# A decoder layer on one core: in the last batch the two layer norms behind the second attention are made per token half

## The reference, cut to what matters

```python
def _layernorm(x, axis=-1, eps=1e-05):
    m = jnp.mean(x, axis=axis, keepdims=True)
    v = jnp.var(x, axis=axis, keepdims=True)
    return (x - m) / jnp.sqrt(v + eps)
...
    x = _layernorm(x + _L0_attn_ref(x, ...), axis=-1)            # block A, gives x1
    x = _layernorm(x + _L0_xattn_ref(x, ctx_2048, ...), axis=-1)  # block B, ends in o @ Wo, gives x2
    x = _layernorm(x + _L0_ffn_ref(x, ...), axis=-1)              # block C, gives the output
...
def _L0_ffn_ref(x, ...):
    result = jnp.einsum('bsd,od->bso', x, base_w) + base_b
    logits = jnp.einsum('bsd,ed->bse', x, router_w) + router_b
    # softmax of 8 experts, the two largest renormalised to a gate of 8 numbers per token
    mid = jnp.einsum('nd,edr->ner', xf, lora_A) * gate[:, :, None]
    return result + 2.0 * jnp.einsum('ner,erd->nd', mid, lora_B)
```

## Time and profile before

| | |
|---|---|
| time, median of 3 runs | 913.03 us (912.97 to 913.53) |
| the profiled execution | 913.3 us, of which its span in the trace is 911.2 us |
| mean granted TensorE clock | 0.986 of full speed |
| PE busy | 802.1 us, 88% of the span |
| DVE, ACT, POOL busy | 509.5, 326.4, 85.5 us |
| instructions | 22548 |

### The profile page before, as it was taken

How to read it: one execution, slowest core, us unless ns; L and a number is a source line. 1 busy time by engine, 2 the same in 40 slices (tenths; PEclk the granted TensorE clock), 3 DMA queues, 4 the chain that set the end, 5 groups by cost and what they waited for, 6 DMA issues and landing times.

```text
span 911.2 us, 22548 instructions
## 1 busy us (share of the span) xinstructions
PE 802.1 (88%) x10161; PEld 524.5 (58%) x10209; DVE 509.5 (56%) x1060; ACT 326.4 (36%) x424; POOL 85.5 (9%) x103
## 2 busy tenths in 40 slices
PE   3788878888998989988998989988998979999996
PEld 2466763477445864577445864577445864486443
DVE  4756584448745593748745593648745582435143
ACT  5534224333245224433245224433245124310422
POOL 1111011000300021000300021000300010010001
PEclk9989999999999999999999999999999999997998
DMA  9921000100002000010002000010001000000000
GB/s 345 246 55 47 2 2 1 47 2 2 2 1 70 3 2 1 26 47 2 1 1 71 3 2 1 27 46 1 1 1 48 2 1 1 24 1 1 1 24 23
DMA packets 19022, 27.10 MB, mean 30 GB/s; under 512 B 5608, under 2 KB 7784, under 8 KB 18928
## 3 DMA queue, kind: packets, MB, share of 16 engines
q1 hardware_dynamic: 18784, 25.64, 9.1%
q10 hardware_dynamic: 144, 0.03, 0.0%
HBM read 21.47 MB, written 4.19 MB: 28 GB/s over the span
## 4 chain that ended last, share of the span: by engine, by line
PE 63%; DVE 19%; ACT 12%; issue 4%; POOL 1%; DMA 1%; ACTq 0%; POOLq 0%; SPq 0%; DVEq 0%
ACT p_b L761 7%; PE ps L1148 7%; PE ps L1184 6%; PE ps L1065 6%; PE ps L1225 6%; DVE max_b L1487 6%; PE ps L1113 4%; PE ps L1048 3%; PE ps L1085 3%; PE ps L893 2%; DVE max_a L1385 2%; PE ps L968 2%; PE ps L1173 2%; PE ps L1157 2%; PE ps L978 2%
## 5 line engine op out<-in xcount | busy, mean ns | idle before, releaser
L761 ACT ACTIVATE p_b<-ps 128x2048 f32<-128x2048 f32 x64 | 106.5, 1664 | 115.9 <-PE ps L1157 115.9
L1487 DVE TENSOR_REDUCE max_b<-ps 128x4 f32<-128x768 f32 (+2 forms) x160 | 106.6, 711 | 31.1 <-PE ps L1127 19.3
L1363 DVE SCALAR_TENSOR_TENSOR nat<-ps,st_a,qkv_bias 128x512 f32<-128x512 f32 x48 | 35.7, 744 | 98.0 <-PE ps L893 96.8
L1113 PE MATMUL ps<-qk_b 32*128 32x192 f32 (+2 forms) x1024 | 65.5, 341 | 22.9 <-DVE max_b L1487 16.8
L1148 PE MATMUL ps<-qk_b 32*128 32x512 f32 (+1 forms) x512 | 66.2, 586 | 9.7 <-ACT p_b L761 5.2
L1113 PEld LDWEIGHTS ps<-qk_b 32*128 32x128 f32 x1024 | 46.2, 188 | 39.9 <-DVE max_b L1487 27.3
L1225 PE MATMUL ps<-base_t,x_t 128*128 128x512 f32 x128 | 63.8, 624 | 0.0
L1173 PE MATMUL ps<-p_b,v_b 128*32 128x256 f32 (+1 forms) x1024 | 61.7, 358 | 2.4 <-ACT p_b L761 2.0
L1048 PE MATMUL ps<-c_t,wq 128*128 128x256 f32 x256 | 60.6, 385 | 2.4 <-DVE out_a L1408 2.3
L1065 PE MATMUL ps<-x_t,wq 128*128 128x256 f32 x256 | 61.3, 385 | 0.0
L1184 PE MATMUL ps<-wo,o_fb 128*128 128x512 f32 x128 | 59.0, 599 | 0.8 <-DVE o_fb L1529 0.8
(11 more groups left out here) (207 smaller groups left out, 1432.7 us busy)
## 6 DMA issues: line engine op xcount, KB each, us to landing
x_in<-x SPq DMA_DIRECT2D x8, 512.0 KB, 5.4
p_b<-ctx SPq DMA_DIRECT2D x8, 512.0 KB, 4.6
y<-x SPq DMA_DIRECT2D x7, 512.0 KB, 3.3
p_b<-L_attn_qkv_w SPq DMA_DIRECT2D x2, 1024.0 KB, 6.5
p_b<-L_xattn_Wq SPq DMA_DIRECT2D x1, 2048.0 KB, 14.9
x<-L_attn_qkv_w SPq DMA_DIRECT2D x2, 512.0 KB, 9.5
x<-L_ffn_base_w SPq DMA_DIRECT2D x2, 512.0 KB, 10.2
wo<-L_xattn_Wo SPq DMA_DIRECT2D x8, 128.0 KB, 9.1
```

The costliest lines, as they stand in the source:

```text
L761: act.activation(p_b[:, j % 2, :, 0:cols], ps[:, 4:8, 0:cols], ACT.Exp, scale=DB ** -0.5).then_inc(pb_here.sem, 1)
L1113: pe.matmul(bank(4 + r)[:, (i % 2) * N:(i % 2) * N + 2 * n * S], q_b[strip[r], i, :, :].rearrange("p h q -> p (h q)"), k_b[strip[r], half, ...
L1363: dve.scalar_tensor_tensor(nat[:, t, w, :], bank(nat_bank(b, w)), st_a[:, 2, t:t + 1], qkv_bias[:, w * C:(w + 1) * C], ALU.mult, ALU.add). ...
L1487: ins = dve.tensor_reduce(max_b[:, half, 0, i:i + k, 2 * n:2 * n + 2], ps[:, 4 + 2 * n:6 + 2 * n, :].rearrange("p r (i n) -> p i r n", i=2 ...
```

## The change

Only batch 7 is changed (`alone(b)` is true for it). For the layer norms of blocks B and C, DVE makes bn_stats, bn_aggr and the variance for one half at a time (`half_stats`), POOL raises one half at a time, and DVE makes the shift of each half (`half_shift`). The order on DVE is now z of half 0, its statistics, then in block B the shift of half 0, z of half 1, its statistics, its shift; in block C z of half 1 stands ahead of the shift of half 0. ACT waits for each half alone, and copies the transposes of half 0 between the two norm applications of block B. PE makes both parts of the Wo product of half 0 ahead of those of half 1, transposes half t of x2 into bank 6 + t, and runs the router product of half 0 between the two groups of transposes. The `keep_on` products ahead of the transposes are 4 and 4, and were 14 and 2.

```diff
@@ POOL b4 (c2 is changed alike, with rs_c)
+                if alone(b):
+                    for t in range(T):
+                        vb_here(pool, b, t + 1)
+                        pool.tensor_tensor(rs_b[:, 1, t:t + 1], rs_b[:, 0, t:t + 1], neghalf[:, 0:1], ALU.pow).then_inc(rb_here.sem, 1)
+                    return
@@ ACT
-                    sh_here(act, b)
+                    sh_here(act, b, t + 1 if alone(b) else None)
...
-                sc_here(act, b)
                 for t in range(T):
+                    sc_here(act, b, t + 1 if alone(b) else None)
...
-                    act.activation(x2_t[:, :, t * P:(t + 1) * P], bank(1).rearrange("p (k n) -> p k n", k=KT),
+                    act.activation(x2_t[:, :, t * P:(t + 1) * P], bank(6 + t if alone(b) else 1).rearrange("p (k n) -> p k n", k=KT),
@@ PE c1_x2, c1
-                    keep_on(b, NB - 1, 2 if t else 14)
+                    keep_on(b, NB - 1, 4)
                     x2_here(pe, b, t + 1)
-                    if t:
+                    if alone(b):
+                        pb_here(pe, b)
+                    elif t:
                         x2t_here(pe, b, 1)
...
-                        mm = pe.transpose(bank(1)[:, k * P:(k + 1) * P], x2[:, t, k * P:(k + 1) * P], eye)
+                        mm = pe.transpose(bank(6 + t if alone(b) else 1)[:, k * P:(k + 1) * P], x2[:, t, k * P:(k + 1) * P], eye)
...
                 keep_on(b, NB - 1, 2)
-                x2t_here(pe, b)
+                if alone(b):
+                    outa_here(pe, b)
+                x2t_here(pe, b, t + 1 if alone(b) else None)
@@ DVE, new helpers
+            def half_stats(c, b, t, z, mv, rs, row, here):
+                c.start(dve, b, 2 * t)
+                c.link(dve.bn_stats(stats[:, t, :], z[:, t, :]))
+                c.link(dve.bn_aggr(mv[:, t, :], stats[:, t, :]))
+                dve.tensor_scalar(rs[:, row, t:t + 1], mv[:, t, 1:2], EPS_LN, None, ALU.add).then_inc(here.sem, 1)
+
+            def half_shift(b, t, mv, rs, row, rstd, done):
+                rstd(dve, b, t + 1)
+                dve.scalar_tensor_tensor(rs[:, row + 2, t:t + 1], mv[:, t, 0:1], -1.0, rs[:, row + 1, t:t + 1], ALU.mult, ALU.mult).then_inc(done.sem, 1)
@@ DVE list, block B and block C of batch 7
-                    (7, of(b4, 0)), (7, of(b4_z, 1)), (7, of(b4, 1)), (7, of(b4, 2)), (7, b4_x2), (7, c1), (7, of(c1_top, 0)), (7, of(c1_top, 1)),
+                    (7, of(b4, 0)), (7, of(b4, 2)), (7, of(b4_z, 1)), (7, of(b4, 1)), (7, b4_x2), (7, c1), (7, of(c1_top, 0)), (7, of(c1_top, 1)),
```

More of the change, by code:

```diff
@@ L411, in program, with alone @@
         NEXT, A, B, C_, D_ = -1, 0, 1, 2, 3
+        def alone(b):
+            return isinstance(b, int) and b == NB - 1
         def apart(b, t):
@@ L585, in c2 @@
             def c2(b):
+                if alone(b):
+                    for t in range(T):
+                        vc_here(pool, b, t + 1)
+                        pool.tensor_tensor(rs_c[:, 1, t:t + 1], rs_c[:, 0, t:t + 1], neghalf[:, 0:1], ALU.pow).then_inc(rc_here.sem, 1)
+                    return
                 vc_here(pool, b)
@@ L793, in _ @@
                     (7, of(b3, 2)), (7, of(b3, 3)), (7, of(b3, 4)), (7, of(b3, 5)), (7, of(b3, 6)), (7, of(b3, 7)), (6, c2_y), (7, of(b4_x2, 0)),
-                    (7, of(b4_x2, 1)), (7, of(c1_x2, 0)), (7, of(c1_x2, 1)), (7, c1), (7, c2), (7, c2_y)]
+                    (7, of(c1_x2, 0)), (7, of(b4_x2, 1)), (7, of(c1_x2, 1)), (7, c1), (7, c2), (7, c2_y)]
             run(act, first, [(C_, of(b3, 3)), (C_, of(b3, 4)), (C_, of(b3, 5)), (C_, of(b3, 6)), (C_, of(b3, 7)), (B, of(b1_qc, 1)), (B, of(b1_k, 0)),
@@ L1216, in c2 @@
                 if half == 0:
-                    if isinstance(b, int) and b == NB - 1:
-                        x2t_here(pe, b)
+                    if alone(b):
+                        x2t_here(pe, b, t + 1)
                         ob_read(pe, b)
@@ L1271, in _ @@
                     (7, of(b3_s, 3)), (7, of(b3_w, 2)), (7, of(b3_s, 4)), (6, of(c2_lora, 1)), (7, of(b3_w, 3)), (7, of(b3_s, 5)), (7, of(b3_w, 4)),
-                    (7, of(b3_s, 6)), (7, of(b3_w, 5)), (7, of(b3_s, 7)), (7, of(b3_w, 6)), (7, of(b3_w, 7)), (7, of(b4, 0, 0)), (7, of(b4, 1, 0)),
-                    (7, of(b4, 0, 1)), (7, of(b4, 1, 1)), (7, of(c1_x2, 0)), (7, of(c1_x2, 1)), (7, of(c1, 0)), (7, of(c1, 1)), (7, of(c2, 0, 0)),
+                    (7, of(b3_s, 6)), (7, of(b3_w, 5)), (7, of(b3_s, 7)), (7, of(b3_w, 6)), (7, of(b3_w, 7)), (7, of(b4, 0, 0)), (7, of(b4, 0, 1)),
+                    (7, of(b4, 1, 0)), (7, of(b4, 1, 1)), (7, of(c1_x2, 0)), (7, of(c1, 0)), (7, of(c1_x2, 1)), (7, of(c1, 1)), (7, of(c2, 0, 0)),
                     (7, of(c2, 0, 1)), (7, of(c2, 1, 0)), (7, c2_gates), (7, of(c2_lora, 0)), (7, of(c2, 1, 1)), (7, of(c2_lora, 1))]
@@ L1536, in b4 @@
             def b4(b, part):
+                if part == T and alone(b):
+                    return half_shift(b, 0, mv_b, rs_b, 0, rb_here, sh_here)
                 c = ch["b4"]; c.start(dve, b, part)
@@ L1539, in b4 @@
                     zb_here(dve, b, part + 1)
+                if alone(b):
+                    return half_stats(c, b, part, x1, mv_b, rs_b, 0, vb_here)
                 norm_stats(c, part, x1, mv_b, rs_b, 0, vb_here)
@@ L1544, in b4_x2 @@
             def b4_x2(b):
+                if alone(b):
+                    return half_shift(b, 1, mv_b, rs_b, 0, rb_here, sh_here)
                 norm_shift(b, mv_b, rs_b, 0, rb_here, sh_here)
@@ L1594, in c2 @@
             def c2(b, part):
+                if part == T and alone(b):
+                    return half_shift(b, 0, mv_c, rs_c, 0, rc_here, sc_here)
                 c = ch["c2"]; c.start(dve, b, part)
@@ L1597, in c2 @@
                     zc_here(dve, b, part + 1)
+                if alone(b):
+                    return half_stats(c, b, part, z_c, mv_c, rs_c, 0, vc_here)
                 norm_stats(c, part, z_c, mv_c, rs_c, 0, vc_here)
@@ L1602, in c2_y @@
             def c2_y(b):
+                if alone(b):
+                    return half_shift(b, 1, mv_c, rs_c, 0, rc_here, sc_here)
                 norm_shift(b, mv_c, rs_c, 0, rc_here, sc_here)
@@ L1640, in _ @@
                     (7, of(b3_on, 0)), (7, of(b3, 1)), (7, of(b3_on, 1)), (7, of(b3_of, 0)), (6, c2_y), (7, of(b3_of, 1)), (7, of(b4_z, 0)),
-                    (7, of(b4, 0)), (7, of(b4_z, 1)), (7, of(b4, 1)), (7, of(b4, 2)), (7, b4_x2), (7, c1), (7, of(c1_top, 0)), (7, of(c1_top, 1)),
-                    (7, of(c1_top, 2)), (7, of(c2_z, 0)), (7, of(c2, 0)), (7, of(c2_z, 1)), (7, of(c2, 1)), (7, of(c2, 2)), (7, c2_y)]
+                    (7, of(b4, 0)), (7, of(b4, 2)), (7, of(b4_z, 1)), (7, of(b4, 1)), (7, b4_x2), (7, c1), (7, of(c1_top, 0)), (7, of(c1_top, 1)),
+                    (7, of(c1_top, 2)), (7, of(c2_z, 0)), (7, of(c2, 0)), (7, of(c2_z, 1)), (7, of(c2, 2)), (7, of(c2, 1)), (7, c2_y)]
             run(dve, first, [(C_, of(b4, 1)), (C_, of(b4, 2)), (C_, b4_x2), (A, of(a2_max, 0)), (A, of(a2_out, 0, 0)), (A, of(a2_out, 0, 1)),
```

## The result

| | before | after |
|---|---|---|
| time, median of 20 runs | 915.22 us (911.13 to 915.94) | 910.4 us (908.71 to 912.53) |
| profiled execution, its span | 913.3, 911.2 us | 911.62, 909.6 us |
| start of the last Wo product to the end of the span | 33.07 us | 29.23 us |

The account below looks back on a forecast made before the run. The prediction took the tail behind the last batch's second attention to be bound by latency, one thread through the engines. Its terms, 2.68 + 0.7 = 3.4 us, gave 909.9 for the profiled execution and 909.6 for the median, range 909.0 to 910.8.

Parts of the forecast that it names:

- The term of the third norm: Last batch's third norm: ACT starts with half 1 instead of taking it second, last output 0.7 us earlier (0.4 to 0.9).
- the sum: Whole kernel: 2.68 + 0.7 = 3.4 us less than the profiled 913.3, so 909.9; 909.6 for the median.
- The second norm to the base product: Last batch, from the second norm's sums: base product starts at 891.64 instead of 894.32, 2.68 us earlier (2.4 to 2.9).
- The lead of half 0: Wo product, half 0's parts first: z of half 0 starts 1.72 us earlier, at 881.87.
- One half's norm: Second norm, from z of one half to ACT: 2.85 us instead of 3.02, with ends 3.02 and 2.75.
- The prediction's half 1: Second norm: x2 ready for PE at 889.01, transposes at 889.26 behind 0.25 of filler, waiting neither for bank 1 nor ACT.
- The end named for a hidden shift: Third norm: upper end of its gain, 0.9 us, if DVE's shift of half 0 is hidden.
- The clock: Rival, tail: with ten filler products gone the clock falls to half, adding 10 us, about 919; chance 0.05.
- DVE was held by POOL: Rival, gate chain: DVE can't proceed beside POOL's additions for 0.7 us, PE waits 0.35, time 910.0; chance 0.1.
- The swap without effect: Rival, Wo product: swapping its parts gives nothing, saving only 1.3 + 0.7 = 2.0 us, time 911.0; chance 0.05.
- the third norm without gain: Rival, third norm: DVE's new shift waits or the transfers end together, time 910.3; chance 0.05.

Follow-up runs that it names:

- e1: The changed kernel with the third norm made for both halves together again, as in the kernel before: tail 30.34 us, base product 13.46 behind the Wo product.
- e3: The changed kernel with the transposes of both halves of x2 in bank 6 instead of 6 and 7: tail 29.19 us.
- e8: The changed kernel with four more POOL additions of 512 columns, results unused, ahead of POOL's own two in the last batch: tail 35.28 us.
- e4: The changed kernel with the Wo product in the old order of parts, (0,0), (1,0), (0,1), (1,1): tail 30.47 us.
- e2: The kernel before with only the third norm made per half; second norm, Wo order, banks and filler as before: tail 31.96 us.
- e12_first_fill: The changed kernel with 5 filler products ahead of the first pair of maxima products, none ahead of half 1's transposes: median 909.86 us, ratio 0.9956.

## Why the prediction was right or wrong

Two steps failed. The term of the third norm was mis-sized: 0.7 in the sum, 1.10 measured. And the sum was hung on a median of 913.03 that doesn't stand for the kernel: over 20 runs it is 915.22. The mechanism of both norms was right.

**The second norm to the base product: right.** 2.68 forecast, 2.74 measured (2.73 alone in e1). The lead of half 0 was 1.72 to the hundredth, its transposes came at the end of the filler, and half 1 waited 0.35 on the filler where 0.25 was forecast. One half's norm took 2.67, not 2.85, but PE's thread over the filler and the router product of half 0 hid that, as the sum said it would. The swap alone carries 1.24 of the gain, and the cut in the filler 2.12; they don't add, as both stand on the one thread over half 0. The banks carry nothing (e3). The prediction's half 1, which waits "neither for bank 1 nor for ACT", doesn't say what removed the wait for bank 1: it was the router product in between.

**The third norm: the mechanism right, the term mis-sized.** 0.7 was forecast, 1.10 measured. From the last sum to ACT it took 2.68 (903.64 to 906.32), where the sum had 3.02 + 0.2 - 0.17 = 3.05. Beside the rows of after stand these two of before:

```profile
905.98 0.17 DVE L1458 TENSOR_SCALAR rs_c<-mv_c 128x2 f32<-128x2 f32 x1
906.23 0.70 POOL L587 TENSOR_TENSOR rs_c<-rs_c,cf 128x2 f32<-128x2 f32 x1 [12.41 <-DVE rs_c L1458]
```

The 0.17 for one bn_aggr less came: from the statistics to the variance it was 1.12 (904.86 to 905.98) and is 0.95 (904.36 to 905.31). The other two figures were wrong. The shift of half 0 was charged with 0.2 and cost nothing: it ran in the shadow of the sum ahead of it (904.25, while the sum ran until 904.33), so that the statistics started 0.72 behind the sum as without it. And POOL's power on one column was taken to cost the same as on two, "since such operations are all start-up"; it took 0.55 instead of 0.70. The end named for a hidden shift, 0.9, was too low by this POOL step.

**The sum: the step to the median failed.** The profile's 913.3 was set against the median of three runs, 913.03, as if these stood for the kernel. Those three all belong to one group of times; over 20 runs the median before is 915.22. So the 3.4 forecast stand against 4.8 between the medians and 3.5 (2.5 to 4.4) by the ratio, while the tail measures 3.84. That the 909.6 lie within 1 us of the measured 910.4 is luck: the start was 2.2 too low and the gain 1.4 too small, and the two errors cancel but for 0.8. Half of the runs after were in the upper group, for which the prediction had no term. It read the clock in the tail and, in 818 to 820, a stretch at half, and did not ask whether that stretch is the same in every execution.

**The rivals.** The clock did not fall in the tail while PE worked, though ten filler products were gone; e8 shows what it costs when PE does idle for 3 us. DVE was held by POOL, once: the third gate operation took 0.21 instead of 0.17 and ended at 894.65, as POOL ended at 894.62. The rule was right, and its price 0.04, hidden, because the base product was the later one. The forecast had POOL end 0.7 behind DVE's start; it was 0.6, and only two operations without a second SBUF input fell into it ahead of the one that was held. The swap without effect and the third norm without gain are refuted by e4 and e2.

## What to carry to other kernels

Where the end of a kernel is one thread through four engines, start at the fork: give the first half all of its matrix product before the second gets any, and move the first half's next product ahead of the second half's wait; and trim the filler to the new, shorter wait, or it eats the gain (2.12 of 2.74 here). Before a forecast of a few tenths of a per cent is set against a median, look along the whole span for stretches at half clock, and take more than three runs: the median of before rose by 2.2 from 3 runs to 20, over half of the change. Filling the stretches was worth about as much as the change itself (3.2 in the kernel before, 913.39 to 910.18).

## What the runs showed of the hardware that was not expected

- POOL's power took 0.55 to 0.56 on 128x1 and 0.69 to 0.71 on 128x2 numbers: even at this size it grew with the number of columns.
- A DVE operation of 16 columns with two SBUF inputs took up to 1.19 instead of 0.17 beside POOL's additions of 1.24, and POOL's own times did not change (2.48 to 2.50 for two). One on a single SBUF input was not slowed (0.17).
- The granted clock fell behind 4 us in which PE was busy for 3.02 (812 to 816, before), and in e12_first_fill behind 3.95 and 3.71 of 4 us (812 to 820), yet it held with 1.10 and 1.34 of 2 us in the tail; so PE's busy time in the rows does not tell when it falls. A product of 512 columns more for each of six pairs, and five more at the idle microsecond, held it.
